# The expert stage of a fused transformer block: each tile adds its share into the rows of `out`, x in three buffers, and no combine stage

## The reference

```
x = x + cross_attention(layernorm(x), ctx)      # 16 heads of 32; 64 batches, 32 queries, 257 keys
x = x + self_attention(layernorm(x))            # rotary, 32 tokens a batch, low-rank keys and values
xf = layernorm(x).reshape(2048, 512)
w, idx = top_k(xf @ Wr, 2);  w = softmax(w)     # 8 experts, two for each token
y[n, e] = (silu(xf[n] @ W1[e]) * (xf[n] @ W3[e])) @ W2[e]      # 512 -> 768 -> 512
out = x + sum over e of y[n, e] * comb[n, e]    # comb: w at the two chosen experts, else 0
```

## Time and profile before

| | |
|---|---|
| median of 3 runs | 1679.87 us (1677.79 to 1682.84) |
| profiled execution, device time | 1679.69 us |
| its span, first to last instruction | 1677.9 us |
| PE busy in the span | 1488.4 us, 89% |
| DVE, ACT, POOL busy | 1089.2, 815.5, 472.4 us |
| experts (first turn of x to last matmul) | 1064.7 to 1640.3 us |
| last matmul to the end of the span | 37.6 us |
| mean granted TensorE clock | 0.952 of 2.4 GHz |

### The profile page before, as it was taken

How to read it: one execution, slowest core, us unless ns; L and a number is a source line. 1 busy time by engine, 2 the same in 40 slices (tenths; PEclk the granted TensorE clock), 3 DMA queues, 4 the chain that set the end, 5 groups by cost and what they waited for, 6 DMA issues and landing times. The chain is left out here.

```text
span 1677.9 us, 40105 instructions
## 1 busy us (share of the span) xinstructions
PE 1488.4 (89%) x15380; PEld 1301.1 (78%) x15380; DVE 1089.2 (65%) x1920; ACT 815.5 (49%) x1520; POOL 472.4 (28%) x717
## 2 busy tenths in 40 slices
PE   5899999999999999978999897688998999999890
PEld 4788888888888888756877775578888989889880
DVE  1566666666566566647786776776676867667674
ACT  3666666666666666543232231335454555545430
POOL 1122222222222221218657675101110110101145
PEclk8999999999999999999999997799999999999995
DMA  8000100000000000000000011537567765776757
GB/s 295 21 26 27 27 25 20 24 25 25 25 25 25 20 24 26 20 1 8 16 21 15 15 59 33 194 139 270 197 224 256 245 235 189 256 248 230 243 168 239
DMA packets 126699, 175.56 MB, mean 105 GB/s; under 512 B 11840, under 2 KB 84480, under 8 KB 126592
## 3 DMA queue, kind: packets, MB, share of 16 engines
q1 hardware_dynamic: 119888, 155.42, 27.5%
q0 software_dynamic: 6704, 18.64, 3.5%
HBM read 155.19 MB, written 18.83 MB: 104 GB/s over the span
## 5 line engine op out<-in xcount | busy, mean ns | idle before, releaser
L1958 DVE TENSOR_TENSOR lo<-raw,hi 128x1024 fp32r<-128x1024 f32 x207 | 246.2, 1220 | 49.0 <-ACT hi L1887 47.8
L1887 ACT CAST hi<-raw 128x1024 fp32r<-128x1024 f32 x207 | 209.2, 1048 | 55.0 <-DMA raw<-in_L_ffn_W_dram 43.1
L52 PE MATMUL mo_bank<-xT_hi,hi 128*128 128x256 f32 x768 | 215.7, 281 | 3.2 <-DVE xT_lo L1967 2.8
L53 PE MATMUL mo_bank<-xT_hi,lo 128*128 128x256 f32 x768 | 214.3, 279 | 0.0
L54 PE MATMUL mo_bank<-xT_lo,hi 128*128 128x256 f32 x768 | 214.1, 279 | 0.0
L534 ACT ACTIVATE Pr<-xa_s,nmax 128x257 f32<-128x257 f32 x256 | 119.1, 473 | 121.9 <-DVE nmax L609 121.9
L576 DVE TENSOR_TENSOR PT_lo<-xa_s,PT_hi 128x512 fp32r<-128x512 f32 x128 | 82.3, 685 | 113.8 <-ACT PT_hi L503 113.8
L52 PEld LDWEIGHTS mo_bank<-xT_hi,hi 128*128 128x128 f32 x768 | 145.9, 190 | 10.2 <-issue 5.9
L52 PE MATMUL xa_s<-zT_hi,QK_hi 128*128 128x258 f32 x512 | 150.0, 293 | 2.4 <-DVE zT_lo L563 1.3
L53 PEld LDWEIGHTS mo_bank<-xT_hi,lo 128*128 128x128 f32 x768 | 145.9, 190 | 2.9
L2043 POOL TENSOR_TENSOR e_carrier<-x_res 128x1 f32<-128x1 f32 x37 | 16.6, 449 | 465.8 <-DMA of_row<-slot_token 465.5
(11 more groups left out here) (315 smaller groups left out, 3896.3 us busy)
## 6 DMA issues: line engine op xcount, KB each, us to landing
raw<-in_L_ffn_W_dram SPq DMA_DIRECT2D x207, 512.0 KB, 8.5
raw<-in_ctx_dram SPq DMA_DIRECT2D x64, 256.0 KB, 2.6
ys<-ysb SPq DMA_DIRECT2D x16, 512.0 KB, 2.6
xs<-xn SPq DMA_DIRECT2D x16, 256.0 KB, 2.0
out_dram<-x_res SPq DMA_DIRECT2D x16, 256.0 KB, 4.3
x_res<-in_x_dram SPq DMA_DIRECT2D x1, 3840.0 KB, 19.0
ys<-ysb SPq DMA_DIRECT2D x7, 256.0 KB, 2.0
raw_o<-in_L_xattn_Wo_dram SPq DMA_DIRECT2D x1, 1024.0 KB, 5.6
```

The lines of the kernel that those rows point to most:

```text
L52: pe.matmul(out, lh, rh, start=start, stop=False)
L53: pe.matmul(out, ll, rh, start=False, stop=False)
L1887: aW.done(act.copy(hi, raw), f"p{c}{q}")
L1958: vW.done(dve.tensor_tensor(lo, raw, hi.bitcast(F32), ALU.subtract), f"p{c}{q}")
```

## The change

What it does, part by part:

- The two words `token number, gate weight` are stored for each place (`slot_val`), where only the token number was. `x_res` is stored to `out` during self attention, and a tile adds its share to the rows of `out` itself: POOL gathers them into `acc`, DVE adds `Y * weight` from PE's banks (`add_share`), POOL scatters them back. `acc` is one buffer, and the gather of a tile waits for the scatter of the one before. `ys`, `ysb`, `find_rows`, `early` and `combine` are gone.
- x has three buffers, one for each `pos`; SP fetches the places of tile n+2 in tile n, after the weights of tile n+1 and once the scatter of tile n-1 has landed, and POOL gathers the x of tile n+2 behind the `acc` gather of tile n.
- `TileTable.fill` goes from the end of self attention into T0, in three parts behind its first three pairs of splits (24 instructions for 29). SP waits for it (`tiles.filled`) before it fetches places and T1's weights.
- All three weight slots of T0 are loaded ahead in self attention (one before). The last four `send`s move behind the barrier.

```
@@ experts, SP
-                def load(t, pos):
...
-                    weights(t, pos, e, range(NS))
-
-                def store(t, pos):
...
+                def places(t, pos, used):
+
+                    rows = CH[pos] * P
+                    row = sp.value_load(table[0:1, 1, slot_of(t, pos)], min_val=0, max_val=n_slot - rows)
+                    if used is not None:
+                        sp.wait_ge(acc_put, 16 * chunks(*used))
...
+                sp.wait_ge(tiles.filled, 1)
                 sp.wait_ge(sent, 32 * (n_tile - 8))
...
+                places(0, 1, None)
+                sp.wait_ge(of_got, 16)
+                places(0, SINGLE, None)
 
                 def tile(t, pos, first, last):
                     if not last:
-                        load(*following(t, pos))
-                    store(t, pos)
+                        weights(*following(t, pos))
+                    if not first and not (isinstance(t, int) and t == N_TRIP):
+                        places(*following(*following(t, pos)), before(t, pos))
@@ experts, PE
                 def y_free(t, pos):
-                    tb, pb = before(t, pos)
-                    aM.wait(pe, tb, f"{pb}y")
-                    if pb != SINGLE:
-                        vM.wait(pe, tb, f"{pb}y")
+                    need(pe, vY, chunks(*before(t, pos)))
@@ experts, DVE
+                def add_share(t, pos):
+                    pM.wait(dve, t, f"{pos}Y{NS - 1 if pos == SINGLE else NH - 1}")
+                    dve.wait_ge(acc_got, 16 * chunks(t, pos))
+                    for r in range(CH[pos]):
+                        dve.scalar_tensor_tensor(acc[:, r, :], bank_y[r][:], of_row[pos][:, r, 1:2].bitcast(F32),
+                                                 acc[:, r, :], ALU.mult, ALU.add).then_inc(vY, 1)
...
+                        if first and j < tiles.FILL_PARTS:
+                            tiles.fill(dve, count, j)
+                        if j == 0 and pos == 0 and not first:
+                            add_share(t - 1, SINGLE)
+                    add_share(t, pos)
                     splits(t, pos, NH, last)
@@ experts, POOL
+                def gather_x(t, pos):
+                    pool.wait_ge(of_got, 16 * index(t, pos))
+                    need(pool, x_got, 16 * (chunks(*before(t, pos)) - 2))
+                    if index(t, pos) > 2:
+                        pX.wait(pool, index(t, pos) - 3, "XT")
+                    carry()
...
+                def gather_acc(t, pos):
+                    need(pool, acc_put, 16 * chunks(*before(t, pos)))
+                    carry()
...
+                def scatter_acc(t, pos):
+                    for c in range(CH[pos]):
+                        pool.wait_ge(vY, chunks(t, pos) - CH[pos] + c + 1)
+                        carry()
...
                 for n in range(1, N_WORK):
...
+                    t, pos = divmod(n, 3)
+                    gather_acc(t, pos)
+                    if n + 2 < N_WORK:
+                        gather_x(*divmod(n + 2, 3))
+                    scatter_acc(t, pos)
```

More of the change, by code:

```diff
@@ L1423, in scratch @@
         self.home = sb("t_home", [P, 2, E])
-        self.lim, self.c1, self.c2 = (sb(n, [P, E]) for n in ("t_lim", "t_c1", "t_c2"))
-        self.ask = [sb(f"t_ask{n}", [P, n_ask]) for n in range(4)]
-        self.moved, self.move = sb("t_moved", [P, n_pick, E]), [sb(f"t_move{n}", [P, n_pick]) for n in range(4)]
-        self.posf, self.less, self.share = (sb(n, [P, n_pick // 2, 2]) for n in ("t_posf", "t_less", "t_share"))
+        self.ask = [sb(f"t_ask{n}", [P, n_ask]) for n in range(2)]
     def chain(self, dve, op):
@@ L1456, in pick_first, with fill @@
         chain(dve.tensor_tensor(turned[:], t[:], d[:], ALU.add))
-    def fill(self, dve, count):
+    FILL_PARTS = 3
+    def fill(self, dve, count, part):
         def chain(op):
@@ L1469, in fill @@
-        chain(dve.tensor_reduce(pairs, self.cmp[:].rearrange("p e (n two) -> p e n two", two=2)[:, :, :, 1], AX_X, ALU.add))
-        chain(dve.tensor_reduce(self.key[:], self.cmp[:], AX_X, ALU.add))
-        chain(dve.scalar_tensor_tensor(singles, pairs, -2.0, self.key[:], ALU.mult, ALU.add))
-        chain(dve.tensor_tensor(self.trip[:], units[:].unsqueeze(2).to_broadcast([P, 2, E, E]),
-                                self.after[2][:].unsqueeze(1).to_broadcast([P, 2, E, E]), ALU.mult))
-        chain(dve.tensor_reduce(ends[:, 0], self.trip[:], AX_X, ALU.add))
@@ L1483, in fill @@
[L1483 to L1485 removed]
+        pairs, singles, (hit, past_in), ask = units[:, 0, :], units[:, 1, :], self.past, self.ask
         def over_experts(t):
             return t[:].rearrange("p k a e -> p k (a e)")
[L1490 removed]
@@ new lines, in fill @@
+        if part == 1:
+            chain(dve.tensor_reduce(one[0][:], ends[:, 0, 0, :], AX_X, ALU.max))
+            chain(dve.tensor_scalar(one[1][:], one[0][:], -float(self.PAIRS), 0.0, ALU.add, ALU.max))
+            chain(dve.tensor_scalar(one[2][:], one[1][:], 2.0, None, ALU.mult))
+            chain(dve.tensor_scalar(ends[:, :, 1, :], ends[:, :, 1, :], one[2][:], None, ALU.add))
+            for past, end in ((hit, 1), (past_in, 0)):
+                chain(dve.tensor_tensor(past[:], ends[:, end].unsqueeze(1).to_broadcast([P, n_ask, 2, E]),
+                                        self.asked[:].unsqueeze(3).to_broadcast([P, n_ask, 2, E]), ALU.is_le))
+            chain(dve.tensor_tensor(hit[:], hit[:], past_in[:], ALU.subtract))
@@ L1745, in _ @@
                 by_tile(sp, tile)
-                sp.wait_ge(y_put, 16 * N_WORK)
             @block.tensor
@@ L2022, in tile @@
                         splits(t, pos, j, last)
-                        if j == NH - 1 and first:
-                            find_rows(dve)
-                            dve.memset(one[:], 1.0).then_inc(rows_found, 1)
-                        if last:
-                            for i in adds.get(j, ()):
-                                add_early(i)
-                    aM.wait(dve, t, f"{pos}y")
-                    need(dve, y_put, 16 * index(t, pos))
-                    vM.done(dve.tensor_copy(ysb[:, 1, :], bank_y[1][:]), f"{pos}y")
+                        if first and j < tiles.FILL_PARTS:
[3 more added lines that the diff above has]
+                    add_share(t, pos)
                     splits(t, pos, NH, last)
```

376 lines of the change are left out of this document (152 added, 224 removed).

## The result

The changed kernel takes 1637.82 us (median of four runs, 1636.78 to 1641.41), the kernel before 1681.36 (four runs, 1677.79 to 1689.29). The ratio is 0.974 with a 95% interval of 0.970 to 0.978. The profiled execution took 1636.78 us, of which 1635.0 is its span; the forecast was 1634.3 of span and 1636 in all.

The account below looks back on a forecast made before the run. PE was taken as the bound, busy 1488.4 of 1677.9 us, so gains come from its gaps. 1677.9 + 0.5 + 0.3 - 9.4 - 4.4 - 30.6 = 1634.3 span, 1636 in all; range 1616 to 1658.

Parts of the forecast that it names:

- The sum: Whole kernel: all terms added to the 1677.9 us span give 1634.3 of span, 1636 in all.
- The single's hole: PE's gap in each single, waiting for x behind SP's stand, closes: 5.1 us a trip, 35.7 in all.
- The new wait: In each first pair PE waits for DVE's add of the single's share behind two splits: 2.1 us a trip.
- The clock: Matmuls after the wait in each first pair run slow for a while: 1.65 us more a trip.
- Rival one: The clock doesn't fall after the wait in first pairs: 11.6 us more gained, 1624.5; chance 25%.
- The chain of acc: POOL's scatters and gather of acc between tiles stay hidden behind PE: cost nothing, 16.6 us against about 20 available.
- Rivals three and four: Acc scatters and gathers land late in the trips: partly late, 1657, 13%; or slower than before, 1690 at 12 each, 5%.
- The start: Start of the experts: 9.7 us from fill and a 6.12 wait are spent on T1's late weights: +0.5.
- The end: T22 and behind the last matmul: T22 loses 4.4 us without early, the stretch behind it 30.6.
- the tail: Behind the last matmul: two adds, a carrier, an issue and a landing take 7.0 us instead of 37.6.
- Rival five: In middle and start, PE waits for weights instead of x, trips keep 71.7 us: 1645; chance 4%.
- Rival two: Start later than worked out, by slower place fetches, table clearing or late weights: with 10 us, 1646; chance 13%.

Follow-up runs that it names:

- before_store_on_act: Kernel before, with only the store of the result ysb issued from ACT's queue instead of SP's; ratio to before 0.987.
- x_one_ahead: Changed kernel with x gathered one tile ahead instead of two, behind the acc gather, three buffers kept; ratio to before 1.013.
- add_first: Changed kernel with the single's share added ahead of part 0's gate product in the next first pair; ratio to before 0.963.
- fill_first: Changed kernel with all three parts of fill on DVE at the start of the experts, ahead of T0's first split; ratio to before 0.968.
- fill_idle: Changed kernel with fill in T0 moved to DVE's idle time, two parts ahead of part 0's gate product, one behind; ratio to before 0.966.
- again: The changed kernel unchanged, run once more on another chip; span 1653.4 us, ratio to before 0.976.

## Why the prediction was right

**The sum** is partly luck. The terms from T0's turning on came out 5.3 us too long against the forecast (0.3, 2.1, 0.3 and 2.6 in the order of the table), and the stretch ahead of it 4.7 us too short. Most of these 4.7 are a difference between executions and not the change (below).

**The single's hole** was forecast at 5.1 us a trip and measured 5.4 (mean of seven singles 20.6 before, 15.1 after). The mechanism was SP's stand at `ysb`: before_store_on_act takes it away alone and gets 3.8 of the 5.4. The forecast gave x three buffers as part of the reason; x_one_ahead and before_store_on_act show that the lead does nothing for x by itself and is the price of having `acc` on the same queue.

**The new wait** was forecast at 2.1 us in each first pair and is 2.10, in seven, at the place the order gave. **The clock** was forecast at 1.65 in each and was 1.5 in six of seven; in the first pairs of before_store_on_act and add_first, without the wait, it isn't there. Rival one (the clock doesn't fall) held in one trip of seven, and in 11 of 42 over all runs with this wait, so "it falls in each" was too strong: with four of seven, as in fill_first, the trips would have been 3 us shorter. The choice of the row in self attention with a wait of the same length was what decided between 1636 and 1624.5.

**What the sum had not**: about 7 us of matmuls that stand further apart. The single's 0.3 more a trip (2.3 us) and the clock's smaller loss (2.5) gave back two thirds: 469.4 forecast, 471.5 measured.

**The chain of acc** was costed at nothing. The working had 16.6 us for two scatters and a gather with their issues. From the carrier (POOL's small operation ahead of each transfer) of the pair's first scatter at 1342.90 to the gather's landing at about 1358.7 (by the median landing) are 15.8, and the add wants it at 1363.7. Rivals three and four had landings of 8 to 12 us in them; the rows show 5.0 for gathers and 6.1 for scatters (medians), 8.5 at most, beside the transfers of weights.

```profile
L2029 POOL DMA_INDIRECT out_dram<-acc,of_row x39: 1019/1810/1859, 1103.8 to 1631.0; - x39
...
DMA to landing us min/median/max: 2.3/6.1/8.5
```

The Trainium skill, "SBUF — State Buffer", section "SBUF: two separate sides", was weighed here: DVE's work can keep POOL from writing descriptors. The traces agree in kind, but at 0.8 us an issue and not at the estimate of 2.5 that comes from the page's figures (about 620 ns alone, about 3100 overlapped). An issue is long when DVE is in the middle of a weight split (`lo`) as it begins, and it then ends 0.83 to 0.93 us behind the end of that split. Here the splits begin at 1343.40, ahead of the scatter:

```profile
1343.40 3.48 DVE L1915 TENSOR_TENSOR lo<-raw,hi 128x1024 fp32r<-128x1024 f32 x3
1343.66 1.84 POOL L2029 DMA_INDIRECT out_dram<-acc,of_row  x1 [0.56 <-POOL e_carrier L1998]
```

In the changed kernel this meets 22 of 39 scatters (1.53 to 1.86 us) and 8 of 39 gathers of `acc` (1.44 to 1.86); all others take 1.00 to 1.23, though DVE was busy with something beside most of these scatters too. Gathers of x never begin inside a split there (0.95 to 0.99 us), but in the kernel before 14 of the 37 do, and those take 1.77 to 1.79 against 0.96 to 1.11. So it goes by the moment of the issue, not by the kind of transfer.

The Trainium skill, "DMA: Bandwidth & Descriptors", section "Anatomy of one DMA — SWDGE (gpsimd) path", gives an estimate of 2.6 us for these transfers. The fastest scatter took 2.3 and the last two, with no weights beside them, 2.8 in the median; but the median of all scatters is 6.1, so with other traffic the rows decide.

**The start** came out by the working that was given: T0's turning to T2 76.8 forecast, 77.1 measured, with late weights for T1 as what eats the gain. fill_first and fill_idle show that it is the place of `fill`: with T1's weights asked for 19.1 and 12.8 us sooner the stretch is 9.9 and 12.5 us shorter. The working left out that `fill` itself holds up T0's gate products, 4.3 of PE's 15.6 us of waits there. What was off is the stretch before: 14.1 us earlier instead of 9.4. The last routing step on DVE began at 1050.14 instead of 1054.36, before fill has any part in it. Of these 4.2 us, 2.9 come between the same two places of self attention: 36.2 us in before (871.2 to 907.4, granted clock 0.95), 33.3 in the changed kernel (870.1 to 903.4, granted clock 1.00), and the run again, which is the changed kernel too, took 37.2 with 0.95. In kernels with the same self attention on one chip the last step began at 1049.4, 1052.0, 1055.9 and 1058.6. So 4 us are within what self attention does from one execution to another, and of the difference of 44 us between the medians about that much may be due to it; in again, on another chip, the medians differ by 40.

**The end** was forecast at 4.4 less in T22 (measured 4.0) and 30.6 less behind it (28.0). The term that was mis-sized is the tail, 7.0 against 9.6: POOL's stand of 3.15 us before its last pair of scatters, once in the program. The tail is 9.4 to 9.6 us in all ten runs of the study that have it, and the stand is in each, 3.15 to 3.21 us. Its cause is open; nothing was tried on it.

**Rival five** (the time goes to weights instead) is ruled out in the trips: no wait of ACT for weights in them. Rival two needed the start to be some 10 us later than worked out; it was 0.3 later and, with what lies ahead of it, 4.4 earlier.

## What to carry to other kernels

A queue that waits in program order for a result holds up what stands behind it, here token numbers and weights: move the wait off that queue first (one edit, 23 us), before buffers or stages are changed. When an add or a copy moves to another engine, look at what stands ahead of it in that engine's row: the same operation cost 3.5 us a trip behind two splits and nothing in front of them. When work leaves a gap between stages for the inside of the next stage, ask what waits for its result: fill gave 10 us by leaving the path and lost them again, mostly through the weights that waited for it. And when a forecast meets the total, check the terms: here errors of 5 us stood on both sides.

## What the runs showed of the hardware

- Waits of PE of 1.96 to 2.25 us were followed by a slow stretch in 31 of 42 cases, waits of 0.83 to 1.69 us in none of 14. The cost was 1.5 us each. In the trip shown above the granted clock is 0.50 from 1366.3 to 1369.3 (1.2 of 2.4 GHz), and the 24 matmuls of the inner product there start within 4.13 us (1366.31 to 1370.44); in the trip without a slow stretch, with the clock at 1.00, within 2.70 (1437.55 to 1440.25).
- The issue of an indirect transfer takes POOL 0.8 us longer when it begins inside a weight split of DVE (1.44 to 1.86 us against 0.95 to 1.23), for gathers and scatters alike.
- Matmuls of 256 columns at the full clock follow each other in 2.63 / 23 = 0.114 us in most of the kernel before and in 2.71 / 23 = 0.118 in the changed one. Both rhythms occur in before_store_on_act. Neither 4 bytes nor a multiple of 64 in the operands' place accounts for it.
- Executions of the same self attention ended up to 13 us apart on one chip, and the changed kernel's 18 us later on a second chip than on the first, with the same times to 0.3 us in each stretch from T0's turning on.
